# A two-layer graph network on one core: statistics and the convolution's y moved to other engines and into PSUM, a reciprocal and a semaphore credit given earlier

## The chip, the cores and the metric

The kernel runs on one core of one Trainium2 chip. The metric is the device time of one execution in microseconds (us), of which the median of three runs is taken. The engines are TensorE (PE in the profile; its weight loads are PEld), VectorE (DVE), ScalarE (ACT), GpSimd (POOL) and SyncE (SP), which only issues DMAs here.

## The reference

Cut to what is computed. There are 6250 nodes of width 512 and 100000 edges; everything is float32.

```python
h = relu(layernorm(x))
for head in range(8):                      # layer 0: graph attention
    feat = h @ W[head]
    logit = leaky_relu(alpha_s[src] + alpha_d[dst], 0.2)
    att = softmax of logit over the edges of one src
    out[head] = relu(segment_sum(att[:, None] * feat[dst], src))
x1 = x + concat(out)
h1 = relu(layernorm(x1))
xn = batchnorm(h1)                         # column sums of h1 and of h1 * h1
agg = segment_sum(xn[src], dst) / max(deg, 1)
conv = relu(agg @ W_conv + b_conv)
y = conv + h_attn + h1                     # h_attn is zero but for 256 nodes
out = x1 + batchnorm(y)                    # column sums of y and of y * y
```

## The kernel before, in words

The nodes lie in 49 tiles of 128 rows. Each engine's stream is written out by hand, and the engines meet only at counting semaphores. The stages follow one another:

1. **Sorts and dense work.** VectorE sorts the edges twice with bitonic networks, sort A by source and sort B by destination (`stage`, `sort_rows`, `sort_crossed`, from line 1904 on). A stage of a sort is one minimum (L1919) and one maximum (L1920) of 512 columns. Merges up to `ROW_BITS` (10) stay in rows; the later ones need a crossing, in which TensorE transposes the keys into PSUM (`cross`, L2062) and VectorE copies half of them back (L1915). Beside it ScalarE and TensorE make the features of layer 0 from the 49 tiles: `make_h` (L1766), transposes (L2075), `project` (L2085, L2090). TensorE's order is fixed: `DENSE_AT` says how many tiles it does before each crossing, so a late tile makes the next crossing late. `make_h` needs the reciprocal of the layer norm's deviation, which VectorE makes in `wait_rstd` (L1956), between the row merges of sort A and those of sort B.
2. **Layer 0.** GpSimd gathers rows of `feat_table` by indirect DMAs (`gather_batch`, L481), 16 for a batch, 55 batches, into `ring`, which holds two batches. Each pair of gathers waits for a credit on the semaphore `lot_ps`, which TensorE raises as it uses up the ring (`lot`, L877). The first `RING_CREDIT` (16) pairs are free: `layer0_tensor` gives them in one `sem_inc` before its first look-up. TensorE comes there after its wait for `sortB_done`, since sort B is still under way when layer 0's own tables are ready. The second half of batch 1 lies over sort B's keys and waits for `sortB_done` by itself (`under_sort`).
3. **x1 and h1.** VectorE makes x1, ScalarE makes h1 (`make_h1`, L589) into four buffers `hout`, SyncE stores them (L466), GpSimd adds h1 to `hsum` (L503), and VectorE squares it (`square_h1`, L793) and adds the square to `hsqsum` (`sum_square`, L796). All of these tensors are in SBUF. TensorE then sums over the rows (L921), and GpSimd clears the accumulator (L1146).
4. **Attention of 256 nodes**, a chain over TensorE, ScalarE and VectorE (L1498 to L1607).
5. **Layer 1.** 832 gathers of `h1_table` (L1161), as many one-hot products (L1616) and as many adds by VectorE (L1414).
6. **Convolution.** For each tile t: VectorE averages (`average`, L1427), TensorE transposes (`turn`, L1626), ScalarE copies back (`turn_out`, L1267), TensorE multiplies by `W_conv` (`convolve`, L1634), VectorE makes y in three operations into `ybuf` in SBUF (`make_y`: L1437, L1440, L1443), ScalarE copies y to `acc` (L1272) and squares it (L1275) (`keep_y`), and GpSimd adds both to column sums (`add_y`, L1177 and L1178). Buffers are double. ScalarE's order is `turn_out(t + 1)`, `keep_y(t)`; TensorE's is `turn(t + 1)`, `convolve(t)`; VectorE's is `average(t + 2)`, `make_y(t)`.
7. **Batch norm and output.**

## Time and profile before

| | us |
|---|---|
| median of 3 runs | 4017.39 |
| lowest, highest of them | 4014.28, 4024.04 |
| the profiled execution | 3989.91 |
| its span | 3988.1 |
| DVE busy | 2676.5 (67%) |
| PE busy | 2692.5 (68%) |
| POOL busy | 1976.9 (50%) |
| ACT busy | 1035.9 (26%) |

The times are of whole executions. The profile is of one execution, and its span runs from the first instruction to the last. It is 27.5 us shorter than the median of the three runs. Starts are counted in us from the span's beginning. A busy share is an average over all seven stages, which have different limits.

### The profile page before, as it was taken

The numbers are of one execution on the slowest core, as the hardware profiler recorded it, in microseconds if no ns is written. First come the engines' busy times: TensorE is split into PE (matmuls) and PEld (weight loads), VectorE is DVE, ScalarE is ACT, GpSimd is POOL, SyncE is SP. The second block draws the span as 40 slices with busy tenths as digits, with TensorE's granted clock in tenths as the row PEclk, the third lists the DMA queues.
The fourth block names the chain that finished last, engine by engine and source line by source line (L and its number), as shares of the span: only waits on it lengthen the run. The fifth ranks groups of instructions, "written<-read, shape, count | busy, mean of one in ns | idle before, by whom it ended". The sixth has DMA issues, their size and how long they took to land. (4 is left out here: it accounts for less than half of the span.)

```text
span 3988.1 us, 46819 instructions
## 1 busy us (share of the span) xinstructions
PE 2692.5 (68%) x10687; PEld 1630.1 (41%) x10688; DVE 2676.5 (67%) x4397; ACT 1035.9 (26%) x3170; POOL 1976.9 (50%) x1977
## 2 busy tenths in 40 slices
PE   0489414777778777777760276777777777778980
PEld 0255213666666666666650152333323233323440
DVE  9798984676667666667679825555555555556777
ACT  8433302444444444444331220000000000000330
POOL 0000006555555555555548614666666666664556
PEclk9999657888888888888885558888888888888995
DMA  4011106666666666666648214566665666663117
GB/s 153 22 47 47 49 0 191 180 189 185 188 181 189 187 185 186 186 187 185 186 142 285 105 45 143 169 178 174 172 178 169 180 172 176 175 174 120 58 55 247
DMA packets 235993, 601.75 MB, mean 151 GB/s; under 512 B 58488, under 2 KB 58488, under 8 KB 235952
## 3 DMA queue, kind: packets, MB, share of 16 engines
q0 software_dynamic: 136960, 456.11, 40.5%
q1 hardware_dynamic: 98992, 145.15, 11.0%
q8 instruction: 18, 0.29, 0.0%
q14 instruction: 23, 0.19, 0.0%
HBM read 547.02 MB, written 54.10 MB: 151 GB/s over the span
## 5 line engine op out<-in xcount | busy, mean ns | idle before, releaser
L481 POOL DMA_INDIRECT big<-feat_table,idx x880 | 838.7, 953 | 1195.5 <-issue 822.8
L1161 POOL DMA_INDIRECT big<-h_table,idx x832 | 788.7, 948 | 573.6 <-issue 358.2
L877 PE MATMUL psA<-big,onehot 128*128 128x260 f32 x1760 | 490.9, 428 | 88.4 <-DVE big L691 69.4
L877 PE MATMUL psB<-big,onehot 128*128 128x260 f32 x1760 | 494.1, 429 | 28.3 <-DVE acc L701 26.2
L547 ACT ACTIVATE big<-big,late_weights 128x65 f32<-128x65 f32 x1760 | 434.5, 344 | 0.0
L877 PEld LDWEIGHTS psA<-big,onehot 128*128 128x128 f32 x1760 | 364.3, 214 | 168.3 <-issue 84.7
L1616 PE MATMUL psA<-big,onehot 128*128 128x512 f32 x556 | 354.0, 722 | 96.8 <-DVE acc L1414 52.9
L1616 PE MATMUL psCD<-big,onehot 128*128 128x512 f32 x554 | 354.8, 726 | 95.2 <-DVE acc L1414 61.7
L1616 PE MATMUL psB<-big,onehot 128*128 128x512 f32 x554 | 350.5, 718 | 94.3 <-DVE acc L1414 58.6
L877 PEld LDWEIGHTS psB<-big,onehot 128*128 128x128 f32 x1760 | 357.1, 213 | 98.5 <-DVE acc L701 38.9
L521 ACT CAST idx<-minorB 128x8 int32 (+1 forms) x107 | 21.5, 204 | 1217.8 <-DMA big<-h_table,idx 1200.4
L1414 DVE TENSOR_TENSOR acc<-acc,psB 128x513 f32 x277 | 191.3, 690 | 185.3 <-remote 60.0
L1414 DVE TENSOR_TENSOR acc<-acc,psCD 128x513 f32 x277 | 191.2, 690 | 183.7 <-remote 77.4
L1414 DVE TENSOR_TENSOR acc<-acc,psA 128x513 f32 x278 | 192.0, 691 | 182.3 <-remote 70.9
L701 DVE TENSOR_TENSOR acc<-acc,psB 128x520 f32 x220 | 152.5, 693 | 82.1 <-PE psA L877 39.2
L691 DVE TENSOR_TENSOR big<-big,psCD 128x1040 f32<-128x1040 f32 x168 | 204.2, 1230 | 3.4 <-issue 3.4
L1919 DVE TENSOR_TENSOR big<-big 128x512 f32<-128x512 f32 x278 | 192.4, 692 | 9.3
L691 DVE TENSOR_TENSOR big<-big,psE 128x1040 f32<-128x1040 f32 x162 | 196.9, 1229 | 0.0
L1634 PE MATMUL psA<-big 128*128 128x512 f32 x392 | 182.8, 610 | 19.3 <-ACT big L1267 19.2
L1920 DVE TENSOR_TENSOR big<-big 128x512 f32<-128x512 f32 x278 | 190.4, 685 | 0.0
L1616 PEld LDWEIGHTS psA<-big,onehot 128*128 128x128 f32 x556 | 96.9, 218 | 213.4 <-issue 112.7
L1616 PEld LDWEIGHTS psCD<-big,onehot 128*128 128x128 f32 x554 | 96.9, 219 | 211.4 <-issue 112.2
(359 smaller groups left out, 3923.2 us busy)
## 6 DMA issues: line engine op xcount, KB each, us to landing
nodes_all<-slot_nodes SPq DMA_DIRECT2D x112, 256.0 KB
big<-feat_table,idx POOLq DMA_INDIRECT x880
big<-h_table,idx POOLq DMA_INDIRECT x832
feat_table<-big SPq DMA_DIRECT2D x49, 264.0 KB, 2.1
x_table<-acc SPq DMA_DIRECT2D x49, 256.0 KB, 3.6
h_table<-big SPq DMA_DIRECT2D x49, 256.0 KB, 2.0
big<-h_table SPq DMA_DIRECT2D x49, 256.0 KB, 2.6
big<-x_table SPq DMA_DIRECT2D x49, 256.0 KB, 3.9
```

The lines of the kernel that those rows point to most:

```text
L481: g.indirect_dma_start(ring[:, b.k, q * SB + u, :], None, feat_table, bass.IndirectOffsetOnAxis(ap=idx[:, 2 * b.k + q, u:u + 1], axis=0)). ...
L521: s.copy(idx[:, q, :], minor_t[:, :, bass.ds(r, 1)].rearrange("p b a -> p (b a)")).then_inc(signal, 1)
L547: ins = s.activation(part, part, ACT.Copy, scale=late_weights[:, at:at + 1])
L691: v.tensor_tensor(pair, pair, weight_ps[b.k][:, 2 * a * H:(2 * a + 2) * H] .rearrange("p (b h) -> p b h", h=H).unsqueeze(3).broadcast_to([ ...
L701: v.tensor_tensor(d, d, (psA, psB)[a % 2][:, :].rearrange("p (u w) -> p u w", u=2)[:, :, 0:HALF_W], ALU.add).then_inc(lot_added, 1)
L877: ins = pet.matmul(psum[:, 512 * hf:512 * hf + HALF_W], onehot[:, q, u % SB, :], ring[:, b.k, u, HALF_W * hf:HALF_W * (hf + 1)], start=(u ...
L1161: g.indirect_dma_start(rows_l1[LOTS * r.place + b // 2][:, b % 2 * D:(b % 2 + 1) * D], None, h1_table, bass.IndirectOffsetOnAxis(ap=idx[:, ...
L1414: v.tensor_tensor(d, d, lot1_sums(r, b)[:, 0:D + 1], ALU.add).then_inc(lot1_added, 1)
L1616: pet.matmul(psum[:, 0:D], onehot[:, r.q, b, :], rows_l1[LOTS * r.place + b // 2][:, b % 2 * D:(b % 2 + 1) * D], start=True, stop=True)
L1634: ins = pet.matmul(psA[:, q * 512:(q + 1) * 512], aggT[:, q, k * P:(k + 1) * P], Wc_s[:, k, :], start=(k == 0), stop=(k == KD - 1))
L1919: v.tensor_tensor(low, a, b, ALU.min).then_inc(srt.step, 1)
L1920: v.tensor_tensor(high, a, b, ALU.max).then_inc(srt.step, 1)
```

## The change

It has four parts.

- **Credit.** `pe.sem_inc(lot_ps, RING_CREDIT)` moves from the head of `layer0_tensor` to the head of TensorE's whole stream.
- **Reciprocal.** Sort A's row merges 7 to 10 are split, and `wait_rstd()` stands ahead of merge 10.
- **Sums of h1.** ScalarE squares h1 after it has made it, with a wait for its own result between. VectorE does both sums, and the two totals are in PSUM (psA and psB); two copies bring them to SBUF at the end. GpSimd has no part in it.
- **y of the convolution.** The first two operations of `make_y` write to PSUM (psB), the third writes `acc` directly, the copy by ScalarE goes away, and GpSimd reads y from `acc`. The bias is read from SBUF, so its copy to PSUM goes. `convolve(t)` waits for the first operation on tile t - 2 rather than for its finished y.

```diff
@@ layer0_gpsimd
-            pool.wait_ge(sums_cleared, 2)
-            def sum_h1(q):
-                g.tensor_tensor(hsum, hsum, hout[:, q, :], ALU.add).then_inc(h_summed, 1)
...
@@ layer0_scalar
+            def square_h1(q):
+                s.activation(hsq[:, q, :], hout[:, q, :], ACT.Square).then_inc(squared, 1)
...
             with act.Fori(1, QUADS) as i:
                 for q in range(4):
                     act.wait_ge(h_summed, i * 4 + (q - 3))
-                    act.wait_ge(squared, i * 4 + (q - 3))
                     act.wait_ge(h1_stored[q], i * 16)
                     act.sem_inc(hold, 1)
                     make_h1(hout[:, q, :], i * 4 + q).then_inc(h1_ready, 1)
+                    act.wait_ge(h1_ready, i * 4 + (q + 1))
+                    act.wait_ge(sq_summed, i * 4 + (q - 3))
+                    act.sem_inc(hold, 1)
+                    square_h1(q)
...
@@ layer0_vector
-            for total in (hsum, hsqsum):
+            for total in (hsum_ps, hsqsum_ps):
                 v.memset(total, 0.0).then_inc(sums_cleared, 1)
-            def square_h1(q):
-                v.tensor_tensor(hsq[:, q, :], hout[:, q, :], hout[:, q, :], ALU.mult).then_inc(squared, 1)
+            def sum_h1(q):
+                v.tensor_tensor(hsum_ps, hsum_ps, hout[:, q, :], ALU.add).then_inc(h_summed, 1)
             def sum_square(q):
-                v.tensor_tensor(hsqsum, hsqsum, hsq[:, q, :], ALU.add).then_inc(sq_summed, 1)
+                v.tensor_tensor(hsqsum_ps, hsqsum_ps, hsq[:, q, :], ALU.add).then_inc(sq_summed, 1)
...
+            dve.wait_ge(h_summed, TILES)
+            v.tensor_copy(hsum, hsum_ps).then_inc(sums_out, 1)
+            dve.wait_ge(sq_summed, TILES)
+            v.tensor_copy(hsqsum, hsqsum_ps).then_inc(sums_out, 1)
             layer1_vector(dve, link, links)
@@ layer0_tensor
-            pe.sem_inc(lot_ps, RING_CREDIT)
             pe.wait_ge(look_ready, 1)
...
-            pe.wait_ge(h_summed, TILES)
-            pe.wait_ge(sq_summed, TILES)
+            pe.wait_ge(sums_out, 2)
@@ layer1_gpsimd
-            def add_y(q, n=P):
-                g.tensor_tensor(ysum[0:n, :], ysum[0:n, :], ybuf[0:n, q, :], ALU.add).then_inc(y_summed, 1)
+            def add_y(t, q, n=P):
+                y = acc[0:n, bass.ds(t, 1), 0:D].rearrange("p a d -> p (a d)")
+                g.tensor_tensor(ysum[0:n, :], ysum[0:n, :], y, ALU.add).then_inc(y_summed, 1)
@@ layer1_scalar, keep_y
-                s.copy(acc[:, bass.ds(t, 1), 0:D].rearrange("p a d -> p (a d)"), ybuf[:, q, :]).then_inc(y_kept, 1)
                 if not first:
                     act.wait_ge(y_summed, t * 2 - 2)
-                s.activation(ysq[:, q, :], ybuf[:, q, :], ACT.Square).then_inc(y_kept, 1)
+                s.activation(ysq[:, q, :], acc[:, bass.ds(t, 1), 0:D].rearrange("p a d -> p (a d)"),
+                             ACT.Square).then_inc(y_kept, 1)
@@ layer1_vector
-            link(v.tensor_copy(bias_ps, bias_rows))
@@ make_y
                 dve.wait_ge(conv_ps, t + 1)
                 if not first:
-                    dve.wait_ge(y_kept, t * 2 - 2)
-                    dve.wait_ge(y_summed, t * 2 - 2)
-                y = ybuf[:, q, :]
-                v.scalar_tensor_tensor(y, shift_rows, indc[:, bass.ds(t, 1)], psA[:, q * 512:(q + 1) * 512], ALU.mult,
-                                       ALU.add).then_inc(y_step, 1)
+                    dve.wait_ge(y_ready, t - 1)
+                v.scalar_tensor_tensor(y_ps[:, q, :], shift_rows, indc[:, bass.ds(t, 1)], psA[:, q * 512:(q + 1) * 512],
+                                       ALU.mult, ALU.add).then_inc(y_step, 1)
                 dve.wait_ge(y_step, t * 2 + 1)
-                v.tensor_tensor(y, y, bias_ps, ALU.add).then_inc(y_step, 1)
+                v.tensor_tensor(y_ps[:, q, :], y_ps[:, q, :], bias_rows, ALU.add).then_inc(y_step, 1)
                 dve.wait_ge(y_step, t * 2 + 2)
                 dve.wait_ge(hc_in[q], loads)
-                return v.scalar_tensor_tensor(y, y, 0.0, h_in[:, q, :], ALU.max, ALU.add)
+                return v.scalar_tensor_tensor(y, y_ps[:, q, :], 0.0, h_in[:, q, :], ALU.max, ALU.add)
@@ layer1_tensor, convolve
-                    pe.wait_ge(y_ready, t - 1)
+                    pe.wait_ge(y_step, t * 2 - 3)
@@ vector block
-            sort_rows(sortA, 7, ROW_BITS)
+            sort_rows(sortA, 7, ROW_BITS - 1)
             wait_rstd()
+            sort_rows(sortA, ROW_BITS, ROW_BITS)
@@ tensor block
+            pe.sem_inc(lot_ps, RING_CREDIT)
             count_pads(1)
```

VectorE, at the end of sort A's row merges, before. The merge of 10 bits is the last ten pairs of L1919 and L1920 ahead of the sign flip (L1927); of them the last two pairs stand here.

```order
L1919 TENSOR_TENSOR big<-big 128x256x2
L1920 TENSOR_TENSOR big<-big 128x256x2
L1919 TENSOR_TENSOR big<-big 128x512
L1920 TENSOR_TENSOR big<-big 128x512
L1927 TENSOR_SCALAR big<-big,signs 128x1024
L1956 RECIPROCAL stat<-stat 128x49
L1957 TENSOR_TENSOR stat<-stat 128x49
```

The same place with the change, from the last stage of merge 9 on (L1916 and L1917 are the minimum and maximum there).

```order
L1916 TENSOR_TENSOR big<-big 128x512
L1917 TENSOR_TENSOR big<-big 128x512
L1953 RECIPROCAL stat<-stat 128x49
L1954 TENSOR_TENSOR stat<-stat 128x49
L1916 TENSOR_TENSOR big<-big 128x512
L1917 TENSOR_TENSOR big<-big 128x512
L1916 TENSOR_TENSOR big<-big 128x2x256
```

The reciprocal and the product after it now stand ahead of twenty minimum and maximum instructions and the flip.

ScalarE in the stage of h1 before: the table load and the square root, then the first tiles (L589 is `make_h1`) and the loop's first turns.

```order
L585 ACT_TABLE_LOAD
L585 ACTIVATE stat<-big,small 128x49
L589 ACTIVATE big<-acc,stat 128x512 x4
L589 ACTIVATE look_space<-acc,stat 128x512 x2
L596 UNCONDITIONAL_BRANCH
L596 ISA
L600 REGISTER_ALU
L589 ISA x2
L589 ACTIVATE big<-acc,stat 128x512
L598 REGISTER_ALU
```

And with the change, inside the loop (L574 is `make_h1`, L578 the square).

```order
L574 ISA x2
L574 ACTIVATE big<-acc,stat 128x512
L592 REGISTER_ALU
L578 ACTIVATE big<-big 128x512
L588 REGISTER_ALU
L574 ISA x2
L574 ACTIVATE big<-acc,stat 128x512
L592 REGISTER_ALU
L578 ACTIVATE big<-big 128x512
```

Each tile has one more ScalarE instruction, and no table load stands between the two kinds.

## Rows read from the trace of the kernel before

**Rows 1.** Timeline, VectorE and ScalarE: start, us, engine, line, operation, [idle before <-releaser]

```profile
137.78 0.69 DVE L1919 TENSOR_TENSOR big<-big 128x512 f32<-128x512 f32 x1
...
151.74 0.46 DVE L1956 RECIPROCAL stat<-stat 128x49 f32<-128x49 f32 x1
...
152.48 1.52 ACT L1766 ACTIVATE big<-acc,stat 128x512 f32<-128x512 f32 x2 [27.26 <-DVE stat L1957]
...
176.74 0.69 DVE L1915 COPY big<-psA 128x512 f32<-128x512 f32 x1 [11.12 <-PE psA L2062]
...
196.48 0.69 DVE L1915 COPY big<-psA 128x512 f32<-128x512 f32 x1 [11.21 <-PE psA L2062]
```

**Rows 2.** Timeline of the end of sort B and the start of layer 0

```profile
487.13 0.81 SPq L408 DMA_DIRECT2D nodes_all<-slot_nodes  x2
...
598.35 1.13 POOL L481 DMA_INDIRECT big<-feat_table,idx  x1 [592.57 <-issue]
...
599.76 0.48 ACT L526 CAST alphas<-psCD 128x384 bf16<-128x384 f32 x1 [115.90 <-PE psCD L828]
...
621.36 0.30 ACT L558 COPY look_space<-big 128x128 f32<-128x128 f32 x1 [21.12 <-DMA big<-feat_table,idx]
...
630.80 0.49 DVE L614 TENSOR_SCALAR big<-nodes_all,iota_col 128x1024 bf16<-128x1024 bf16 x1 [5.56 <-remote]
...
636.32 0.19 DVE L660 TENSOR_TENSOR look_space<-psCD,chunk_of 128x32 f32<-128x32 f32 x1 [5.03 <-remote]
...
645.08 3.83 PE L877 MATMUL psA<-big,onehot 128*128 128x260 f32 x8 [5.41 <-DVE big L691]
```

**Rows 3.** Groups of instructions, 2150 to 2275 us: xcount | busy us, mean ns | idle before

```profile
L503 POOL TENSOR_TENSOR big<-big 128x512 f32<-128x512 f32 x49 | 75.9, 1550 | 41.0 <-ACT big L589 27.3 <-DVE big L790 9.6 <-POOL big L503 0.7
L793 DVE TENSOR_TENSOR big<-big 128x512 f32<-128x512 f32 x49 | 65.3, 1335 | 0.5 <-ACT big L589 0.5
L796 DVE TENSOR_TENSOR big<-big 128x512 f32<-128x512 f32 x49 | 53.6, 1094 | 0.1
L589 ACT ACTIVATE big<-acc,stat 128x512 f32 (+1 forms) x49 | 39.3, 814 | 67.1 <-DVE big L793 60.9 <-DMA h_table<-big 5.4 <-DVE stat L787 0.8
```

**Rows 4.** Groups of instructions, 3640 to 3905 us, the convolution

```profile
L1634 PE MATMUL psA<-big 128*128 128x512 f32 x392 | 182.8, 610 | 19.3 <-ACT big L1267 19.2
L1443 DVE SCALAR_TENSOR_TENSOR big<-big 128x512 f32<-128x512 f32 x49 | 74.2, 1515 | 4.0
L1437 DVE SCALAR_TENSOR_TENSOR big<-big,stat,psA 128x512 f32<-128x512 f32 x49 | 36.6, 747 | 53.1 <-ACT onehot L1275 29.7 <-PE psA L1634 22.8 <-ACT acc L1272 0.6
L1440 DVE TENSOR_TENSOR big<-big,psCD 128x512 f32<-128x512 f32 x49 | 33.6, 686 | 1.7
L1275 ACT ACTIVATE onehot<-big 128x512 f32<-128x512 f32 x49 | 30.7, 627 | 0.0
L1272 ACT COPY acc<-big 128x512 f32 (+1 forms) x49 | 30.4, 620 | 146.6 <-DVE big L1443 135.3 <-DVE big L1449 11.4
L1626 PE MATMUL psCD<-ident_wide,big 128*128 128x128 f32 x196 | 30.2, 279 | 3.9 <-DVE big L1427 3.9
L1474 DVE TENSOR_TENSOR psB<-big 128x512 f32<-128x512 f32 x1 | 0.7, 699 | 0.0
```

**Rows 5.** Timeline of two tiles of the convolution

```profile
3753.34 0.62 ACT L1272 COPY acc<-big 128x512 f32 x1 [2.94 <-DVE big L1443]
...
3755.10 3.69 PE L1634 MATMUL psA<-big 128*128 128x512 f32 x8 [0.50 <-ACT big L1267]
...
3762.47 0.62 ACT L1272 COPY acc<-big 128x512 f32 x1 [2.94 <-DVE big L1443]
```

**Rows 6.** Timeline: a ScalarE self-wait, and first and last of the h1 stage

```profile
171.64 0.20 ACT L1782 COPY big<-alphas 128x8 f32 x1 [0.27 <-ACT alphas L1777]
...
2165.84 2.94 ACT L589 ACTIVATE big<-acc,stat 128x512 f32 x4 [4.96 <-DMA h_table<-big]
...
2270.03 3.54 PE L921 MATMUL psCD<-ones,big 128*128 128x1 f32 x16 [196.15 <-DVE big L796]
```

**Rows 7.** VectorE's L667 over all batches: durations in ns, least/median/most

```profile
L667 DVE TENSOR_TENSOR look_space<-alphas x55: 291/291/293, 637.7 to 2054.8; 128x128 f32<-128x128 f32 x55
```

More of the change, by code:

```diff
@@ L401, in build @@
         hsum, hsqsum = rows[:, 0, :], rows[:, 1, :]
+        hsum_ps, hsqsum_ps = psA[:, 0:D], psB[:, 0:D]
+        sums_out = sem("sums_out")
         QUADS = TILES // 4
@@ L498, in layer0_gpsimd @@
                 scale_sums(t)
-            pool.wait_ge(sums_cleared, 2)
-            def sum_h1(q):
-                g.tensor_tensor(hsum, hsum, hout[:, q, :], ALU.add).then_inc(h_summed, 1)
-            for q in range(4):
-                pool.wait_ge(h1_ready, q + 1)
-                if q > 0:
-                    pool.wait_ge(h_summed, q)
-                sum_h1(q)
-            with pool.Fori(1, QUADS) as i:
-                for q in range(4):
-                    pool.wait_ge(h1_ready, i * 4 + (q + 1))
-                    pool.wait_ge(h_summed, i * 4 + q)
-                    sum_h1(q)
-            pool.wait_ge(h1_ready, TILES)
-            pool.wait_ge(h_summed, TILES - 1)
-            sum_h1(0)
             layer1_gpsimd(pool)
@@ L607, in layer0_scalar @@
             make_h1(hout[:, 0, :], TILES - 1).then_inc(h1_ready, 1)
+            act.wait_ge(h1_ready, TILES)
+            act.wait_ge(sq_summed, TILES - 4)
+            square_h1(0)
             layer1_scalar(act, link, links, put_indices)
@@ L799, in layer0_vector @@
                 dve.wait_ge(h1_ready, q + 1)
-                square_h1(q)
                 if q > 0:
-                    dve.wait_ge(squared, q)
-                    if q > 1:
-                        dve.wait_ge(sq_summed, q - 1)
-                    sum_square(q - 1)
+                    dve.wait_ge(h_summed, q)
+                sum_h1(q)
+                dve.wait_ge(squared, q + 1)
+                if q > 0:
+                    dve.wait_ge(sq_summed, q)
+                sum_square(q)
             with dve.Fori(1, QUADS) as i:
@@ L808, in layer0_vector @@
                     dve.wait_ge(h1_ready, i * 4 + (q + 1))
-                    square_h1(q)
-                    dve.wait_ge(squared, i * 4 + q)
-                    dve.wait_ge(sq_summed, i * 4 + (q - 1))
-                    sum_square((q - 1) % 4)
-            dve.wait_ge(h1_ready, TILES)
-            square_h1(0)
-            for t in (TILES - 2, TILES - 1):
-                dve.wait_ge(squared, t + 1)
-                dve.wait_ge(sq_summed, t)
-                sum_square(t % 4)
+                    dve.wait_ge(h_summed, i * 4 + q)
+                    sum_h1(q)
+                    dve.wait_ge(squared, i * 4 + (q + 1))
+                    dve.wait_ge(sq_summed, i * 4 + q)
+                    sum_square(q)
+            dve.wait_ge(h1_ready, TILES)
+            dve.wait_ge(h_summed, TILES - 1)
+            sum_h1(0)
+            dve.wait_ge(squared, TILES)
+            dve.wait_ge(sq_summed, TILES - 1)
+            sum_square(0)
+            dve.wait_ge(h_summed, TILES)
+            v.tensor_copy(hsum, hsum_ps).then_inc(sums_out, 1)
+            dve.wait_ge(sq_summed, TILES)
+            v.tensor_copy(hsqsum, hsqsum_ps).then_inc(sums_out, 1)
             layer1_vector(dve, link, links)
@@ L1180, in layer1_gpsimd @@
                 for q in range(2):
-                    pool.wait_ge(y_kept, i * 4 + (2 * q + 2))
+                    pool.wait_ge(y_kept, i * 2 + (q + 1))
                     pool.sem_inc(hold, 1)
-                    add_y(q)
+                    add_y(i * 2 + q, q)
                     pool.wait_ge(y_summed, i * 4 + (2 * q + 2))
                     pool.sem_inc(hold, 1)
-            pool.wait_ge(y_kept, 2 * TILES)
-            add_y(0, LAST)
+            pool.wait_ge(y_kept, TILES)
+            add_y(TILES - 1, 0, LAST)
             def add_x1(t, q, loads, stores):
```

11 lines of the change are left out of this document (6 added, 5 removed).

## The prediction

> **What bounds the kernel now.** No engine is busy for more than 68% of the span, because the stages follow one another and each has its own limit. So each part of the change is priced in its own stage, and what it takes off there comes off the end: nothing but the order of stages lies behind it. I read the timeline at the borders of the stages, then the groups of instructions of the two stages that are rebuilt, then the timeline again for who waits for whom.
>
> In the sort stage VectorE works without a gap except where TensorE is late with a crossing. [rows 1] show the start of it: ScalarE has been idle for 27.26 us when the reciprocal at 151.74 lets it make the first tile, and 24 us later VectorE stands 11.12 us, then 11.21 us, for crossings that TensorE gives only after its tiles. At the start of layer 0 everything stands 21.12 us for the first batch of gathers, which GpSimd begins at 598.35 [rows 2]. In the stage of h1 VectorE is the bound: its two operations take 65.3 + 53.6 = 118.9 us, and ScalarE is idle for 67.1 us, most of it behind VectorE's squares [rows 3]. In the convolution no engine is full: TensorE is idle for 19.3 + 3.9 = 23.2 us [rows 4], and the loop closes over three engines [rows 5].
>
> **The reciprocal.** Merge 10 begins at 137.78 and the reciprocal now comes at 151.74 [rows 1]; it moves ahead by 13.96 us. It adds no wait: ScalarE's 27.26 us of idle time before 152.48 put the end of the statistics at 125.2, before 137.78. TensorE's tiles and so its crossings come 14.0 us sooner, while VectorE arrives at the first crossing when it did before. So the first stop of 11.12 us goes, and of the second, 11.21 us, there remain 11.21 - (13.96 - 11.12) = 8.4 us. From there on both engines run 14.0 us ahead, and the later stops keep their lengths. **-14.0 us.** The bounds: 11.1 us if only the first stop goes, 14.0 us at most.
>
> **The credit.** GpSimd's other waits are met when SyncE, which waits for the same stored slots, issues its loads at 487.13 [rows 2]. So 24 of the first 32 gathers (the second half of batch 1 waits for sort B) run under sort B, 110 us before they do now. ScalarE was ready at 599.76 + 0.48 = 600.24 and took the first batch at 621.36 [rows 2]: 21.1 us go. Behind that lie two stops of VectorE of 5.56 and 5.03 us with a remote releaser, in the middle of a stretch in which GpSimd issues gathers without a break, before the first product at 645.08 [rows 2]. With 8 gathers left instead of 32 I let half of these 10.6 us go, 5.3 us. **-26.4 us**, between 21.1 and 31.7 if the sort is not touched. What hides the 24 gathers is sort B; its cost if it is touched is the first rival. What is late next is the chain from 600.24 to the first product, which is VectorE's, ScalarE's and TensorE's short steps. Later batches are paced by credits as now.
>
> **The sums of h1.** GpSimd loses 49 additions (75.9 us busy), VectorE loses 49 squares and gets 49 additions, ScalarE gets 49 squares [rows 3]. VectorE's squares last 1335 ns and its additions 1094 ns on average, both with two SBUF inputs beside GpSimd's, where the same kind of operation takes 690 ns alone (L1919 in [rows 1]). The new ones take one operand from PSUM and write to PSUM. No row has both; L1440 reads PSUM in 686 ns and L1474 writes it in 699 ns [rows 4], each like SBUF, so I take 0.69 us, and 1.38 us a tile. The other end is that reading and writing do not overlap: 0.686 + 0.699 = 1.385 us each. ScalarE needs per tile `make_h1` 0.814 us [rows 3], the wait for its own result, 0.27 us between two such instructions in [rows 6], and the square, 0.627 us like L1275 [rows 4]: 1.71 us, and I allow 0.04 for the registers: 1.75 us. So ScalarE is the new bound, behind it VectorE and the store.
>
> The fifth tile still waits for the store of the first and starts at 2165.84 [rows 6]. 44 further tiles by 1.75 us are 77.0 us, to 2242.8; then 0.81 + 0.27 + 0.63 + 0.69 for the last tile, 0.7 for the copy that is not overlapped, and 0.5 for handing over: 2246.4, where the column sums on TensorE now start at 2270.03 [rows 6]. **-23.6 us.** At 1.44 us a tile (no gap at all) it would be 37.2 us; with 1.385 us per VectorE operation, 2.77 us a tile, 21.3 us would be lost. The attention and GpSimd's clearing start from the same events as before, and sooner.
>
> ScalarE: Activation LUTs, a page of the Trainium skill, says in its rules for kernel authors that multiplications and additions belong on VectorE and not on ScalarE. By that rule the square stays on VectorE, three operations by 0.69 us, 2.07 us a tile, and this part would bring 9.5 us instead of 23.6. The rows speak for the change all the same, since ScalarE has 67.1 idle us there and VectorE has 0.6.
>
> **y of the convolution.** The copy of the bias goes, some 0.7 us before the first tile. In the loop, y of one tile lets ScalarE copy and square it, only then bring the next transposed tile back, then TensorE convolve, then VectorE make y two tiles on: 3762.47 - 3753.34 = 9.13 us for two tiles [rows 5]. The copy, 0.62 us, goes. L1443, 1.515 us with two SBUF inputs beside GpSimd's additions, gets a PSUM operand and should take 0.747 us like L1437, which runs beside the same additions: 0.77 us less [rows 4]. The chain becomes 9.13 - 0.62 - 0.77 = 7.74 us, 3.87 us a tile against 4.56. But TensorE can't follow so far: its idle 23.2 us are 0.47 us a tile, which leaves 4.09 us a tile. So TensorE becomes the bound and the gain is 22 of the 23.2 us. The looser wait of `convolve` is worth nothing then. **-22.7 us** with the bias. The bounds: 33.8 + 0.7 us if the modelled ends of matmuls hide some room (49 by 0.69), and 0 if the two PSUM operations take 1.385 us each, which puts the 1.39 us back.
>
> **The sum.** 14.0 + 26.4 + 23.6 + 22.7 = 86.7 us. Against the profiled execution's 3989.9 us this is 3903.2. The median of the three runs stands 27.5 us above that execution, and I put the change on it: 4017.4 - 86.7 = 3930.7, so 3931 us. That the profiled execution lies so far below the three runs is the larger doubt of the low end.
>
> **Rivals.**
>
> *The gathers hold up sort B, or start no sooner.* Sort B is nearly all minima and maxima with two SBUF inputs. If each of 24 gathers made one of them as long as L793 (1335 against 690 ns), that is 15.5 us, and two stops like those at 630.80 and 636.32 are 10.6 us: 26.1 us, and the credit brings nothing. The same comes out if GpSimd's last wait is another than the credit; the profile puts its 592.57 us down to "issue" and names none [rows 2]. 3931 + 26 = 3957 us. Against it: L667, with two SBUF inputs, took 291 to 293 ns in all 55 batches, beside gathers in most of them [rows 7]. 13%.
>
> Runtime: NRT & Kernel Launch, in the Trainium skill, says under instruction fetch mechanics that straight code is fetched ahead and a page boundary is mostly hidden. By that page, if the remote stops are code loading, a sort of straight code would lose none of the 10.6 us; the stops in [rows 2] lie in straight code too, so the trace does not bear it out under gathers.
>
> *The convolution or h1 gain only half.* ScalarE's order ties `turn_out` to the square, and a self-wait can cost more than 0.27 us. Half of 23.6 + 22.7 is lost: 3931 + 23 = 3954 us. For it: both new bounds are computed from parts and neither has been seen. 12%.
>
> *More is gained.* The remote stops go wholly, TensorE runs at 3.87 us a tile and ScalarE at 1.6: 5.3 + 11 + 6.6 more, 3908 us. 12%.
>
> *Slower: the operations on PSUM in place.* Let one of them, 98 in the stage of h1 and 98 in the convolution, take p us. The h1 part then gains 100.6 - 88p (VectorE bounds) and the convolution 24.5 by (2.77 - 2p); with 41.1 us from the rest the sum is 209.6 - 137p. It is zero at p = 1.53. At p = 2.03, a slow SBUF read of 1.335 and an unshared write of 0.699, it is -68.5, 4086 us. Against it: L1440 and L1474 show neither side dearer, and L1440 stands beside GpSimd's additions at 686 ns. 4%.
>
> **How the numbers follow.** The forecast has 59%. The range should take in the rivals at 3957, 3954 and 3908, and for the low end the level of the profiled execution, 3903, with some of the larger gain: 3890 to 3966. A difference of 0.3%, 12 us, is about the least that a measurement of this kernel can tell. Every case but the last is faster by far more. Faster 0.95, within 0.3% 0.02, slower 0.03: part of the last rival's 4% lies between.
>
> **What would show it.** Right: the reciprocal near 138 us and a first stop of VectorE at L1915's place below 1 us, the second near 8.4; the first gather near 473, the first product 35 to 46 us sooner than at 645.08; VectorE's sums at 0.69 us, ScalarE's pitch at 1.75 us a tile, the column sums of h1 64 us earlier in all than at 2270.03; L1443's successor at 0.75 us and the convolution at 4.09 us a tile with TensorE nearly without idle time. Wrong: gaps or longer minima in sort B while gathers are issued; PSUM operations above 1.2 us; ScalarE's idle time growing in the h1 stage; stops with a remote releaser in new places.

## The result and the profile after

The changed kernel takes 3911.41 us (median of four runs, 3897.95 to 3918.14), the kernel before 4017.49 us beside it (four runs, 4014.28 to 4024.04). The ratio is 0.9738, 95% interval 0.972 to 0.9755: 106 us faster, where 3931 us had been predicted, 86.7 us faster. The profiled execution took 3897.95 us, span 3896.2 us, so the two profiled executions are only 92 us apart. The one before lay 27.5 us below its median, this one 13.5.

Timeline of VectorE and ScalarE in the sort, after. L1953 is the reciprocal, L1763 `make_h`, L1912 the copy behind a crossing; they answer to [rows 1].

```profile
137.66 0.46 DVE L1953 RECIPROCAL stat<-stat 128x49 f32<-128x49 f32 x1
...
138.39 0.82 ACT L1763 ACTIVATE big<-acc,stat 128x512 f32<-128x512 f32 x1 [13.10 <-DVE stat L1954]
...
165.40 0.68 DVE L1912 COPY big<-psA 128x512 f32<-128x512 f32 x1
...
183.18 0.69 DVE L1912 COPY big<-psA 128x512 f32<-128x512 f32 x1 [9.23 <-PE psA L2060]
```

The first stop has gone, and of the second 9.23 us remain. Sort B ends at 584.2 instead of 597.1 us.

Timeline of the start of layer 0, after, for [rows 2].

```profile
474.98 1.13 POOL L483 DMA_INDIRECT big<-feat_table,idx  x1 [469.20 <-issue]
...
585.10 0.95 POOL L483 DMA_INDIRECT big<-feat_table,idx  x1 [78.27 <-issue]
...
587.57 0.30 ACT L543 COPY look_space<-big 128x128 f32<-128x128 f32 x1
...
592.25 0.27 ACT L545 COPY alphas<-psCD 128x128 f32<-128x128 f32 x1 [4.37 <-remote]
...
601.92 1.66 PE L878 MATMUL psA<-big,onehot 128*128 128x260 f32 x3 [1.50 <-DVE big L686]
```

The gathers begin 109 us before the end of sort B, ScalarE's L543 has no wait at all (it had 21.12 us), and the first product comes at 601.92 instead of 645.08.

Groups of instructions in the stage of h1, 2105 to 2195 us, after, for [rows 3].

```profile
L574 ACT ACTIVATE big<-acc,stat 128x512 f32 (+1 forms) x49 | 39.4, 804 | 3.7 <-DMA h_table<-big 2.3 <-DVE stat L782 0.8
L788 DVE TENSOR_TENSOR psA<-psA,big 128x512 f32<-128x512 f32 x49 | 34.3, 700 | 5.8 <-ACT big L574 5.6
L791 DVE TENSOR_TENSOR psB<-psB,big 128x512 f32<-128x512 f32 x49 | 34.3, 699 | 3.1
L578 ACT ACTIVATE big<-big 128x512 f32<-128x512 f32 x49 | 30.9, 632 | 6.3
```

ScalarE's idle time before `make_h1` (L574) has fallen from 67.1 to 3.7 us, with 6.3 us more before the squares (L578): ScalarE is now nearly full. The timeline shows one tile of it, and the column sums at the end of the stage ([rows 6] before).

```profile
2165.85 0.80 ACT L574 ACTIVATE big<-acc,stat 128x512 f32 x1
2165.98 0.70 DVE L791 TENSOR_TENSOR psB<-psB,big 128x512 f32<-128x512 f32 x1
2166.68 0.70 DVE L788 TENSOR_TENSOR psA<-psA,big 128x512 f32<-128x512 f32 x1
2166.79 0.63 ACT L578 ACTIVATE big<-big 128x512 f32<-128x512 f32 x1
2167.33 0.80 ACT L574 ACTIVATE big<-acc,stat 128x512 f32 x1
...
2190.45 1.87 PE L920 MATMUL psCD<-ones,big 128*128 128x1 f32 x8 [161.80 <-DVE big L819]
```

`make_h1` to the next one is 1.48 us: 0.94 to the start of the square, 0.54 from there. With the loop's branch in every fourth tile it is 66.6 us for 44 tiles, 1.51 us a tile. The first four tiles stand ahead of the loop, written out one by one, and are faster: 0.83 us to the square and 0.54 from there, 1.37 us a tile.

```profile
2112.44 0.80 ACT L574 ACTIVATE big<-acc,stat 128x512 f32<-128x512 f32 x1
2113.27 0.63 ACT L578 ACTIVATE big<-big 128x512 f32<-128x512 f32 x1
2113.81 0.80 ACT L574 ACTIVATE big<-acc,stat 128x512 f32<-128x512 f32 x1
```

Groups of instructions in the convolution, 3590 to 3810 us, after, for [rows 4].

```profile
L1631 PE MATMUL psA<-big 128*128 128x512 f32 x392 | 180.6, 604 | 0.0
...
L1434 DVE SCALAR_TENSOR_TENSOR psB<-big,stat,psA 128x512 f32<-128x512 f32 x49 | 37.0, 756 | 60.6 <-PE psA L1631 60.6
L1437 DVE TENSOR_TENSOR psB<-psB,big 128x512 f32<-128x512 f32 x49 | 34.3, 699 | 1.7
L1440 DVE SCALAR_TENSOR_TENSOR acc<-psB,big 128x512 f32 (+1 forms) x49 | 33.9, 692 | 9.2 <-DVE psB L1437 5.7
...
L1623 PE MATMUL psCD<-ident_wide,big 128*128 128x128 f32 x196 | 30.2, 278 | 3.6 <-DVE big L1425 3.6
```

TensorE waits for nothing in front of its products (L1631), and VectorE waits 60.6 us for TensorE alone. The third operation (L1440) fell from 1515 to 692 ns. The same place of the loop comes round every 7.88 us, two tiles:

```profile
3660.78 3.60 PE L1631 MATMUL psA<-big 128*128 128x512 f32 x8
...
3668.66 3.60 PE L1631 MATMUL psA<-big 128*128 128x512 f32 x8
```

Set side by side, the stages of the two profiled executions are these (us, the stage's own length, from the starts of the rows named).

| stage | before | after | predicted |
|---|---|---|---|
| start to end of sort B | 597.1 | 584.2 (-12.9) | -14.0 |
| to layer 0's first product | 48.0 | 17.7 (-30.3) | -26.4 |
| first to last product of layer 0 | 1428.4 | 1426.4 (-2.0) | 0 |
| first `make_h1` to the column sums | 113.5 | 79.3 (-34.2) | -23.6 |
| column sums to layer 1's first addition | 152.8 | 151.5 (-1.3) | 0 |
| layer 1, first to last addition | 1234.8 | 1252.8 (**+18.0**) | 0 |
| to the first y | 11.2 | 10.4 (-0.8) | -0.7 |
| first to last y | 216.6 | 189.0 (-27.6) | -22.0 |

The four parts give 105.8 us. An unchanged stage, layer 1, takes 18.0 back in this pair of executions. The experiments had to settle four things: whether each part brings what the table says, why h1 gained more than predicted, which half of the convolution's part works, and what layer 1 has to do with it.

### The profile page after: what moved, and what is told of

Same layout as the page of the kernel before. It is cut to its first block and busy times, and to the rows that moved or that the text cites. A ratio compares the mean times of both kernels' runs of the same rounds, so it can differ in the third digit from the quotient of the medians.

```text
span 3896.2 us, 46842 instructions
## 1 busy us (share of the span) xinstructions
PE 2683.0 (69%) x10687; PEld 1624.5 (42%) x10688; DVE 2594.5 (67%) x4398; ACT 1038.9 (27%) x3170; POOL 1898.3 (49%) x1928
## 3 DMA queue, kind: packets, MB, share of 16 engines
q1 hardware_dynamic: 98992, 145.15, 11.2%
## 5 line engine op out<-in xcount | busy, mean ns | idle before, releaser
L878 PE MATMUL psB<-big,onehot 128*128 128x260 f32 x1760 | 513.2, 442 | 49.1 <-DVE acc L696 45.8
L878 PE MATMUL psA<-big,onehot 128*128 128x260 f32 x1760 | 459.8, 407 | 37.1 <-DVE big L686 21.4
L878 PEld LDWEIGHTS psB<-big,onehot 128*128 128x128 f32 x1760 | 365.4, 218 | 131.2 <-DVE acc L696 69.2
L878 PEld LDWEIGHTS psA<-big,onehot 128*128 128x128 f32 x1760 | 348.2, 204 | 104.8 <-issue 32.8
L696 DVE TENSOR_TENSOR acc<-acc,psB 128x520 f32 x220 | 152.5, 693 | 106.1 <-PE psA L878 63.7
L1916 DVE TENSOR_TENSOR big<-big 128x512 f32<-128x512 f32 x278 | 192.4, 692 | 9.3
L1917 DVE TENSOR_TENSOR big<-big 128x512 f32<-128x512 f32 x278 | 190.6, 685 | 0.0
L1613 PEld LDWEIGHTS psA<-big,onehot 128*128 128x128 f32 x556 | 96.1, 217 | 219.4 <-DVE acc L1413 109.8
L1613 PEld LDWEIGHTS psB<-big,onehot 128*128 128x128 f32 x554 | 95.5, 216 | 216.0 <-issue 115.3
```

Source lines behind the costliest of these rows:

```text
L696: v.tensor_tensor(d, d, (psA, psB)[a % 2][:, :].rearrange("p (u w) -> p u w", u=2)[:, :, 0:HALF_W], ALU.add).then_inc(lot_added, 1)
L878: ins = pet.matmul(psum[:, 512 * hf:512 * hf + HALF_W], onehot[:, q, u % SB, :], ring[:, b.k, u, HALF_W * hf:HALF_W * (hf + 1)], start=(u ...
L1613: pet.matmul(psum[:, 0:D], onehot[:, r.q, b, :], rows_l1[LOTS * r.place + b // 2][:, b % 2 * D:(b % 2 + 1) * D], start=True, stop=True)
L1916: v.tensor_tensor(low, a, b, ALU.min).then_inc(srt.step, 1)
L1917: v.tensor_tensor(high, a, b, ALU.max).then_inc(srt.step, 1)
```

## The experiments

All of them were measured later, on four chips (numbers 5, 14, 15 and 3), and on each of them the kernel before takes 3447 to 3453 us instead of 4017. The chip of the first pair of kernels is not known, so whether the 570 us more there belong to another chip or to another condition stays open. Each ratio below is to the kernel before as measured on the same chip. "Change" is the first run below, 3346.50 us on chip 5, where the kernel before took 3447.33. The changed kernel was not measured on the other chips. There the kernel before took 3446.72 (chip 14), 3452.58 (chip 15) and 3452.81 us (chip 3), so a difference to the change across chips can be off by some 5 us, and the lengths of stages decide.

**The changed kernel once more.** No edit.

> The changed kernel itself once more, unedited. Between the first product of layer 1 and its end, the changed kernel's trace shows 1255.8 us where the kernel before had 1238.1, though no instruction of that stage was touched. Theory: this is the spread of single executions (VectorE's idle time with a remote releaser was 244 us against 208). Then this second profile may lie anywhere between some 1235 and 1260 us there, while the sort, the stage of h1 (79.3 us from the start of h1 to the column sums) and the convolution (189.0 us from first to last tile) repeat within 1 us. Rival: the changed code lies differently in memory and is fetched less well; then the stage is again 1255.8 us within 3. Ratio to the kernel before 0.974 in either case.

Measured: 3346.50 us (3342.83 to 3355.35), the kernel before 3447.33; ratio 0.9698, interval 0.9678 to 0.9718, 100.8 us faster. The expected ratio, 0.974, lies outside that interval. The sort (583.2), the stage of h1 (79.1) and the convolution (188.9) repeat the first pair's lengths within 1 us. The gathering stages don't: layer 0 takes 1123.8 instead of 1426.4 us, layer 1 1023.4 instead of 1252.8. Two views show what differs. In the waits of the first profile of the changed kernel there stand, among others,

```profile
DVE acc L1413 <- remote: 244.1, 81, 5.0
...
DVE big L609 <- remote: 150.7, 45, 6.7
...
POOL big L1159 <- remote: 107.5, 34, 3.7
```

(us in total, times, the longest), and in the second profile of the same kernel no wait with a remote releaser stands among the 200 longest entries. And in layer 1 the granted clock was 0.84 in the first pair and 1.00 here (of the windows, first 2350 to 3590 us of the first profile, then 2040 to 3040 us of the second; after the length come the busy times of TensorE, its weight loads, VectorE, ScalarE and GpSimd, then the granted clock, the DMAs' share and GB/s):

```profile
2350.00:3590.00 1240.00, 952.33 (x2461) 371.54 (x2459) 674.58 (x922) 20.68 (x101) 763.03 (x806) 0.84 0.60 171
```

```profile
2040.00:3040.00 1000.00, 817.71 (x2434) 323.89 (x2433) 666.08 (x914) 20.38 (x100) 756.48 (x800) 1.00 0.72 210
```

Neither the theory nor the rival on layer 1 had that in mind, and this run decides between them only for its own conditions. Over all twelve kernels measured later, in which the code ahead of layer 1 has nine different forms, the stage took 1021.5 to 1024.4 us: where the remote stops are absent, the position of the code costs no more than these 3 us. The 18.0 us belong to the first pair, where VectorE's stops with a remote releaser in front of layer 1's additions added up to 208 us in the kernel before and 244 us in the changed one. No kernel was profiled twice under those conditions. So it stays open whether the 18.0 us are the spread of single executions or the rival's worse fetching of the changed code.

**The credit back.**

```diff
@@ tensor block
-            pe.sem_inc(lot_ps, RING_CREDIT)
@@ layer0_tensor
+            pe.sem_inc(lot_ps, RING_CREDIT)
             pe.wait_ge(look_ready, 1)
```

> The changed kernel with TensorE's credit of the gathers given at the head of layer 0 again. Theory: the first gather starts some 590 us in instead of 475, the first products of layer 0 come 30 us later against the end of sort B than in the changed kernel (21 us of waiting for the batch, 9 to 10 us of stops with a remote releaser that come back), and the time rises by 30 us, ratio to the kernel before 0.981. Rival, my prediction's term: only half of the remote stops went because of the credit, the time rises by 26 us. Second rival: the remote stops have nothing to do with the gathers; then they stay away and it rises by 21 us.

Measured: 3367.67 us, ratio 0.9762 (0.9743 to 0.9782), 21 us more than the change. From the end of sort B to the first product it takes 33.6 us instead of 13.5. The timeline of this kernel:

```profile
585.53 1.12 POOL L483 DMA_INDIRECT big<-feat_table,idx  x1 [579.76 <-issue]
...
608.22 0.30 ACT L543 COPY look_space<-big 128x128 f32<-128x128 f32 x1 [20.82 <-DMA big<-feat_table,idx]
```

The wait is 20.82 us, where [rows 2] have 21.12. GpSimd issues gathers without a break from 585.53 on, and still VectorE has no stop with a remote releaser. So the second rival's 21 us is what was measured, but only because these stops don't occur at all under these conditions. Where they do occur they are VectorE's 5.56 + 5.03 us [rows 2] before, and ScalarE's 4.37 us with the change. The lengths from the end of sort B to the first product say what they cost: 48.0 us before against 33.6 here, both without the early credit, and 17.7 us with the change against 13.5. So of the 30.3 us of the first pair 20.1 are the wait for the batch and 10.2 go with the remote stops.

**The credit alone**, on the kernel before.

```diff
@@ layer0_tensor of the kernel before
-            pe.sem_inc(lot_ps, RING_CREDIT)
@@ tensor block of the kernel before
+            pe.sem_inc(lot_ps, RING_CREDIT)
             count_pads(1)
```

> The kernel before with the credit alone moved to the head of TensorE's stream. Where the kernel before takes about 3450 us, as in the other runs of this study, VectorE has no stops with a remote releaser at the start of layer 0, and undoing the credit cost 21 us; the theory is then that the credit alone brings the same, 20 to 21 us, ratio 0.994. Where the kernel before takes about 4017 us, as in the first comparison, such stops are there, and the first product should come 30 us sooner if they go with the gathers, 21 us if they stay. Rival: the gain of the credit needs the other parts, because something else is late in the kernel before; then less than 15 us in either case.

Measured: 3430.03 us, ratio 0.9936 (0.992 to 0.9953), 22.8 us less than the kernel before. From the end of sort B to the first product it takes 13.7 us, sort B ends at 596.9 like before (597.1), and layer 0 from first to last product takes 1121.3. The part needs no other, and sort B is not touched by the 24 gathers. The pair with the early reciprocal says the same: sort B ends at 584.3 us in the kernel without them (the credit back) and at 583.2 in the changed kernel.

**The reciprocal back.**

```diff
-            sort_rows(sortA, 7, ROW_BITS - 1)
+            sort_rows(sortA, 7, ROW_BITS)
             wait_rstd()
-            sort_rows(sortA, ROW_BITS, ROW_BITS)
```

> The changed kernel with the reciprocal behind merge 10 again. Theory: the reciprocal comes at 151.7 instead of 137.6 us, VectorE stands 11.1 us at the first crossing and 11.2 at the second (instead of 0 and 9.2), and sort B ends 12.9 us later. Rival, my prediction's term: 14.0 us later.

Measured: 3359.01 us, ratio 0.9743 (0.9727 to 0.9759), 12.5 us more than the change. Sort B ends at 597.3 us, against 582.8 to 585.0 in the nine other kernels of this study with the early reciprocal and the old order of tiles. So the part is worth 12.3 to 14.5 us, and this spread is too wide to tell 12.9 from 14.0. The stops are back:

```profile
176.93 0.69 DVE L1912 COPY big<-psA 128x512 f32<-128x512 f32 x1 [11.35 <-PE psA L2059]
...
196.67 0.69 DVE L1912 COPY big<-psA 128x512 f32<-128x512 f32 x1 [11.21 <-PE psA L2059]
```

**The sums of h1 back.**

```diff
+            pool.wait_ge(sums_cleared, 2)
+            def sum_h1(q):
+                g.tensor_tensor(hsum, hsum, hout[:, q, :], ALU.add).then_inc(h_summed, 1)
...
-                s.activation(hsq[:, q, :], hout[:, q, :], ACT.Square).then_inc(squared, 1)
...
+                v.tensor_tensor(hsq[:, q, :], hout[:, q, :], hout[:, q, :], ALU.mult).then_inc(squared, 1)
```

> The changed kernel with the sums of h1 as before: GpSimd adds h1, VectorE squares and adds the squares, all in SBUF. Theory: from the start of the stage of h1 to the column sums it takes 113.5 us again instead of 79.3, VectorE's square 1335 ns and its addition 1094 ns, so 34 us more, ratio 0.9823. Rival: part of the 34 us came from the earlier credit or the different start; then less than 30 us.

Measured: 3381.10 us, ratio 0.9801 (0.9779 to 0.9823), 34.6 us more than the change, and 113.6 us in the stage. VectorE's groups in it are as slow as in [rows 3]:

```profile
L795 DVE TENSOR_TENSOR big<-big 128x512 f32<-128x512 f32 x49 | 65.3, 1334 | 0.6 <-ACT big L591 0.6
L798 DVE TENSOR_TENSOR big<-big 128x512 f32<-128x512 f32 x49 | 53.6, 1093 | 0.1
```

**The convolution's part back**, as in the diff of the change, reversed.

> The changed kernel with the convolution's y as before: y in SBUF, ScalarE copies and squares it, the next product waits for the finished y, the bias copied to PSUM. Theory: 4.51 us a tile instead of 3.94 and 0.8 us ahead of the first, so 29 us more, ratio 0.981. If the four parts are independent, the sum of the four undone parts is 12.9 + 30 + 34 + 29 = 106 us, which is the difference of the two medians, and layer 1 has no part in it; if layer 1 really lost 17.7 us, the sum of the undone parts is larger by that than the whole.

Measured: 3372.94 us, ratio 0.9776 (0.9757 to 0.9796), 26.4 us more than the change; 216.4 us from first to last y instead of 188.9, and 0.8 us more ahead of them. The four undone parts are 21.2 + 12.5 + 34.6 + 26.4 = 94.7 us (the second from chip 14, the others from chip 5), the whole change is 100.8 us on chip 5. Six us are within what four differences of medians can be off: from the column sums to layer 1's first addition alone, which no part touches, the twelve kernels took 141.6 to 146.2 us. Within that the parts are independent, and no hidden loss shows beside them.

**The square on VectorE.** The order of operations for a tile is square, sum of h1, sum of squares, the totals in PSUM, and GpSimd has no part.

```diff
-                    act.wait_ge(h1_ready, i * 4 + (q + 1))
-                    act.wait_ge(sq_summed, i * 4 + (q - 3))
-                    square_h1(q)
...
                     dve.wait_ge(h1_ready, i * 4 + (q + 1))
+                    square_h1(q)
```

The page that the expectation speaks of is ScalarE: Activation LUTs of the Trainium skill, whose rule the prediction weighed.

> The changed kernel with the square of h1 on VectorE (three VectorE operations for a tile, sums in PSUM, GpSimd idle, ScalarE only makes h1), the way the page on ScalarE would have it. Theory: VectorE is the bound at 3 x 0.69 = 2.07 to 2.10 us a tile instead of 1.51, so from the start of the stage of h1 to the column sums 79.2 + 44 x 0.58 = 105 us, 26 us more than the change. Rival: without GpSimd, the square costs less than an addition, or ScalarE's square was hidden by something else; then less than 20 us more.

Measured: 3360.09 us, ratio 0.9749 (0.9733 to 0.9765); the stage takes 92.8 us, 13.7 more than the change and not 26. The rival is right, for a reason that it did not name. VectorE's three operations of one tile, in this kernel's timeline:

```profile
1824.41 0.68 DVE L783 TENSOR_TENSOR big<-big 128x512 f32<-128x512 f32 x1
1825.01 0.69 DVE L778 TENSOR_TENSOR psA<-psA,big 128x512 f32<-128x512 f32 x1
1825.61 0.69 DVE L781 TENSOR_TENSOR psB<-psB,big 128x512 f32<-128x512 f32 x1
...
1826.20 0.68 DVE L783 TENSOR_TENSOR big<-big 128x512 f32<-128x512 f32 x1
```

Each record lasts 0.68 to 0.69 us, but they start 0.60 us apart: 1.80 us a tile, not 2.07. In these rows the records overlap, and no operation there waits for the result of the one just before it. The run also splits the part: 113.6 - 92.8 = 20.8 us come from taking GpSimd away, 13.7 from ScalarE's square. With the square left on VectorE the part would have brought 20.8 us instead of 34.5, where the prediction had computed 9.5 for that case. That is the placement which the rule of ScalarE: Activation LUTs in the Trainium skill asks for (multiplications and additions belong on VectorE). The runs don't bear it out here: ScalarE had 67.1 us to spare [rows 3], and its square made the stage 13.7 us shorter.

**The totals in SBUF.**

```diff
-        hsum_ps, hsqsum_ps = psA[:, 0:D], psB[:, 0:D]
+        hsum_ps, hsqsum_ps = hsum, hsqsum
...
-            v.tensor_copy(hsum, hsum_ps).then_inc(sums_out, 1)
+            dve.sem_inc(sums_out, 1)
```

> The changed kernel with the two totals of h1 in SBUF instead of PSUM, all else as changed (ScalarE squares, VectorE adds both, GpSimd has no part; the two copies at the end fall away). Theory: PSUM is not what makes VectorE's additions fast, GpSimd's absence is: the additions take 0.69 to 0.70 us in SBUF too, ScalarE stays the bound at 1.51 us a tile, and the stage gets 1.4 us shorter by the two copies, which is no difference that the ratio shows. Rival: two SBUF operands are dear by themselves (1.09 us and more, as before); then VectorE is the bound at 2.2 us a tile or more and the stage takes 30 us more.

Measured: 3346.19 us, the change's 3346.50; ratio 0.9707 (0.9691 to 0.9723); the stage takes 78.0 us, 1.1 less. The additions, with both inputs and the output in SBUF, in the groups of this kernel:

```profile
L791 DVE TENSOR_TENSOR big<-big 128x512 f32<-128x512 f32 x49 | 33.9, 692 | 3.4
L788 DVE TENSOR_TENSOR big<-big 128x512 f32<-128x512 f32 x49 | 33.9, 692 | 6.0 <-ACT big L574 5.5
```

692 ns, where the same addition took 1093 beside GpSimd's. PSUM has no part in the gain of this stage.

**The square late.** ScalarE makes tile t, then squares tile t - 1.

```diff
                     make_h1(hout[:, q, :], i * 4 + q).then_inc(h1_ready, 1)
-                    act.wait_ge(h1_ready, i * 4 + (q + 1))
+                    act.wait_ge(h1_ready, i * 4 + q)
                     act.wait_ge(sq_summed, i * 4 + (q - 3))
                     act.sem_inc(hold, 1)
-                    square_h1(q)
+                    square_h1((q - 1) % 4)
```

> The changed kernel with ScalarE's square of a tile issued behind the making of the next tile, so that it never waits for its own result. Theory: ScalarE's 1.51 us a tile are 0.80 + 0.15 of waiting for itself + 0.53 and a little for the loop; without the 0.15 ScalarE needs 1.36, and VectorE with 2 x 0.70 = 1.40 becomes the bound: 44 x 0.11 = 5 us less in the stage of h1, about the least that a ratio can tell, so read it from the stage. Rival: the next square starts no sooner because VectorE's own order or the store of h1 sets the pace at 1.51; then no gain.

Measured: 3335.69 us, ratio 0.9676 (0.9655 to 0.9697), 10.8 us less than the change; the stage takes 67.6 us, 11.5 less. It is twice the 5 us expected:

```profile
1825.77 0.80 ACT L574 ACTIVATE big<-acc,stat 128x512 f32 x1
1825.90 0.70 DVE L796 TENSOR_TENSOR psB<-psB,big 128x512 f32<-128x512 f32 x1
1826.47 0.61 ACT L578 ACTIVATE big<-big 128x512 f32<-128x512 f32 x1
1826.51 0.69 DVE L793 TENSOR_TENSOR psA<-psA,big 128x512 f32<-128x512 f32 x1
1826.99 0.80 ACT L574 ACTIVATE big<-acc,stat 128x512 f32 x1
```

The tile takes 1.22 us. ScalarE's two records of 0.80 and 0.61 us start 0.70 and 0.52 apart, VectorE's of 0.70 and 0.69 0.61 apart. In the changed kernel the square started 0.94 us behind `make_h1`, 0.24 us later than here, though the records leave a gap of only 0.14. Not all of the 0.24 is the wait for its own result: in the four tiles ahead of the loop, which have the same wait, the square starts after 0.83 us, 0.13 later than here. The other 0.11 us come only in the loop, where further semaphore waits and register instructions stand between the two; no run tells which of them costs it.

**The copy kept**, with y of the first two operations in PSUM.

```diff
-                y = acc[:, bass.ds(t, 1), 0:D].rearrange("p a d -> p (a d)")
+                y = ybuf[:, q, :]
...
+                s.copy(acc[:, bass.ds(t, 1), 0:D].rearrange("p a d -> p (a d)"), ybuf[:, q, :]).then_inc(y_kept, 1)
```

> The changed kernel with one half of the convolution's part undone: the first two operations on y stay in PSUM, but the third writes a buffer in SBUF, which ScalarE copies to the accumulator and squares, as before. Theory: the chain of two tiles was 9.13 us; only the 0.77 us of the third operation is saved, so 8.36 us, 4.18 us a tile against 3.94 with both halves (and 4.51 with none): 48 x 0.24 = 11.5 us more than the change. Rival: the copy had been hidden and the whole gain is VectorE's third operation; then 3.94 and no difference.

Measured: 3360.20 us against the kernel before at 3452.58, ratio 0.973 (0.9714 to 0.9747). From first to last y 198.6 us, 4.14 a tile and 9.7 us more than the change.

**y in SBUF**, without the copy.

```diff
-        y_ps = psB[:, :].rearrange("p (q d) -> p q d", q=2)
+        bias_ps = psD[:, :]
+        y_ps = rowsf[:, 6 * D:8 * D].rearrange("p (q d) -> p q d", q=2)
```

> The changed kernel with the other half undone: ScalarE's copy stays away and the third operation writes the accumulator, but y of the first two operations lies in SBUF again. Theory: the third operation has two SBUF inputs beside GpSimd's additions and takes 1.5 us again instead of 0.69; the chain is 9.13 - 0.62 = 8.51 us, 4.25 us a tile, with the copy of the bias 48 x 0.31 + 0.7 = 15.6 us more than the change. Rival, from the stage of h1, where the totals in SBUF cost no more than in PSUM: here too only GpSimd's neighbourhood matters and it now comes at another time; then the third operation takes 0.7 to 0.9 us and nothing is lost.

Measured: 3362.98 us, ratio 0.9746 (0.973 to 0.9762). From first to last y 201.6 us, 4.20 a tile and 12.7 us more than the change. The third operation (durations in ns, least, median, most; its instructions by line):

```profile
L1442 DVE SCALAR_TENSOR_TENSOR acc<-big x49: 691/1433/1732, 3055.8 to 3257.4; 128x512 f32 x44, 128x512 f32<-128x512 f32 x5
```

Beside GpSimd's additions two SBUF inputs cost 1433 ns in the middle. The least, 691 ns, was reached in the first tile, whose operation starts at 3055.8, before GpSimd's first addition at 3058.2. Both theories hold within 0.05 us a tile. Of the 27.5 us, dropping the copy without PSUM brings 216.4 - 201.6 = 14.8 and PSUM with the copy 216.4 - 198.6 = 17.8; together not 32.6, because TensorE's 3.94 us a tile stop them. Both kernels keep the looser wait of `convolve`, so either number may hold a share of it, and no run undoes that wait alone.

**A version that beats both.** The late square, and TensorE's tiles laid differently between the crossings.

```diff
-        DENSE_AT = (2, 4, 4, 2, 4, 2, 4) + (1, 3, 3, 1, 3, 0, 3, 3, 0, 3, 3, 0, 1, 0)
+        DENSE_AT = (1, 3, 3, 2, 4, 4, 3) + (3, 0, 2, 2, 3, 0, 3, 1, 2, 2, 3, 3, 1, 1)
```

> The changed kernel with the late square of h1, and in the sort stage with TensorE's tiles laid differently between the crossings: 1, 3, 3, 2, 4, 4, 3 and 3, 0, 2, 2, 3, 0, 3, 1, 2, 2, 3, 3, 1, 1 instead of 2, 4, 4, 2, 4, 2, 4 and 1, 3, 3, 1, 3, 0, 3, 3, 0, 3, 3, 0, 1, 0. Theory: VectorE's stops for crossings in the changed kernel add up to 22.6 us beside psA (9.2, 10.4, 2.7 and small ones) while TensorE is idle for 51 us in the same stage, so at 4.7 us a tile the tiles fit behind the crossings that VectorE reaches late: sort B ends 22 us sooner, near 562. With 11 us from the late square 33 us in all, ratio to the kernel before 0.960. Rival: TensorE's idle time comes when the inputs of its tiles are not made or its buffers are not free, or the crossings need more slack than the trace shows: half of it, ratio 0.963 to 0.965.

Measured: 3315.80 us (3314.07 to 3318.5), the kernel before 3452.58; ratio 0.9608 (0.9592 to 0.9624), 31 us less than the change on chip 5. Sort B ends at 561.1 instead of 583.2 us. VectorE's copies behind crossings wait for almost nothing any more (its groups from 137 to 436 us; in the changed kernel the first of them had 22.6 us):

```profile
L1917 DVE COPY big<-psA 128x512 f32<-128x512 f32 x14 | 9.6, 684 | 0.4 <-PE psA L2065 0.4
L1917 DVE COPY big<-psCD 128x512 f32<-128x512 f32 x7 | 4.8, 685 | 0.0
```

## Why the prediction was right, and where it was short

The prediction had the sign, the mechanism of each part and their order, and its 3931 us is 20 us above the measured 3911. The sum of 86.7 us was short by 19.1 of the four parts' 105.8 us. That the profiled pair lies 92 us apart, close to 86.7, is luck: the 18.0 us that layer 1 took more in that execution hide most of the shortfall.

- **The reciprocal**, -14.0: 12.9 us in the first pair. Of the second stop 9.23 us remained, not 8.4: TensorE's second crossing let VectorE go on at 183.18 instead of 196.48, 13.3 us sooner and not 14.0.
- **The credit**, -26.4: 30.3 us in the first pair, 20 to 23 where no remote stops occur (20.1 in the stage, 21.2 and 22.8 between medians). That confirms the term of 21.1 us for the wait. The term "half of these 10.6 us" was a choice without a reason behind the half; some 10 us went. What makes these stops stays open. The runs show that gathers issued without a break are not enough to cause them. The conditions in which they occur did not come back, and no run tests the code loading that the prediction names as a possible cause.
- **The sums of h1**, -23.6: 34.2 us. This is the largest error, and it is a size. The step that failed is "0.814, the wait for its own result, 0.27, and the square, 0.627 ... 1.75 us". Measured are 0.94 us from `make_h1` to the square, 0.54 from the square to the next `make_h1`, and 1.51 with the branch. 44 times 0.24 us are 10.6 us, which is the whole error of the term. It has two halves. The gap between `make_h1` and the square was put at 0.27 us, from a small copy in [rows 6], and is 0.14. And the square with the registers was put at 0.67 us as if the next instruction started where this one ended; it starts after 0.54. The loop's branch takes 0.03 of this back. VectorE's two sums were 0.70 us each as predicted, and ScalarE was the bound as predicted.
- **y of the convolution**, -22.7: 27.6 + 0.8 = 28.4 us. TensorE became the bound as predicted, but at 3.94 us a tile and not at 4.09. The step that was short was to read its idle time of 0.47 us a tile as all that it could give (over 48 tiles that is 22.6 us, where the sum has 22.0). The time fell from 4.51 to 3.94 us a tile, by 0.57. The prediction's own bound, that the modelled ends of matmuls hide some room, was the better reading; the price of the chain, 3.87, was nearly reached. That "the looser wait of `convolve` is worth nothing" was not tested.
- **What was put at nothing.** Layer 0 and the attention moved by 2.0 and 1.3 us. Layer 1 took 18.0 us more in this pair of executions, and the twelve kernels measured later show a spread of 3 us. The medians' 106.1 us agree with the four parts' 105.8 us and not with the 92 us of the profiled pair; that fits a loss of layer 1 in that one execution, but does not show it.

Of the rivals, "more is gained", 3908 us, came nearest to the measured 3911: the start of layer 0 lost 10.2 us with the remote stops, where the rival had 10.6, TensorE ran at 3.94 us a tile instead of its 3.87 and ScalarE at 1.51 instead of its 1.6. "The gathers hold up sort B" fell: sort B ends at 596.9 with 24 gathers beside it and at 597.1 without. "Slower by operations on PSUM in place" fell too: they take 699 to 700 ns, and 692 in SBUF. "By half" fell with the two undone parts, 34.6 and 26.4 us.

One reason in the prediction was wrong though its number held. PSUM was given as what makes VectorE's additions of h1 short. It is GpSimd's absence; only in the convolution, where GpSimd goes on adding, does PSUM matter.

## What to carry to other kernels

Where GpSimd and VectorE both stream tensors from SBUF, ask first whether GpSimd's share can go elsewhere (here the addition fell from 1093 to 692 ns), and use PSUM for an operand where it can't (from 1515 to 692 ns). Price a chain of short instructions on one engine by their distance from start to start in a row where they stand back to back, not by their durations; here a wait of an instruction for the one just before it broke this overlap, and issuing another tile's instruction in between restored it, for 11.5 us. After a change that makes one engine early, look again at how the other engine's work is laid between the meeting points: here 22 us lay in one line of numbers.

## What was not expected of the hardware

- **Records overlap.** VectorE's operations of 0.68 to 0.70 us on 128 x 512 started 0.60 to 0.61 us apart, ScalarE's of 0.80 and 0.61 us 0.70 and 0.52 us apart, when they did not depend on the one just before.
- **The same addition** took 692 ns in SBUF, 699 to 700 with its total in PSUM, and 1093 in SBUF beside GpSimd's. VectorE's square took 678 ns without GpSimd's additions and 1334 beside them. The third operation on y with two SBUF inputs took 691 and 1433 ns.
- **The gathering stages changed and the others did not.** Layer 0 took 1426 to 1428 us and layer 1 1235 to 1253 in the first pair, with waits of VectorE, ScalarE and GpSimd on remote releasers and a granted clock of 0.84 in the changed kernel's layer 1; later 1119 to 1124 and 1022 to 1024, on four chips, with none of these waits and a clock of 1.00 in layer 1. The same kernel's stages of h1 and the convolution agree within 0.3 us between the two. What the two conditions are stays open.
- **GpSimd's issues of gathers** beside sort B took up to 1.43 us instead of 0.95, and the minima and maxima beside them did not get longer (691 to 694 and 680 to 687 ns).
